# Routing after attention: the order of projection and router products on TensorE, and a reduction split in two on VectorE

## The reference

```python
qkv = (x @ Wqkv + bqkv)                      # 16 heads of 16
scores = q @ k.T / sqrt(16) - slope * |i - j|
x = layernorm(x + softmax(scores) @ v @ Wout + bout)

weights = softmax(x @ router_w.T + router_b)            # 8 experts
topk_vals, topk_idx = top_k(weights, 2)
expert_mask = (topk_flat > 0)[:, :-1]
sorted_indices = argsort(-expert_mask, axis=0)[:cap]    # cap = 512 tokens an expert
inputs = x_flat[used_idx] * sorted_mask
h = relu(inputs @ experts_inter)                        # 256 -> 1024
out = (h @ experts_out) * in_w
x = layernorm(x + scatter_add(out) + x * noop_weight)
```

## Time and profile before

| | |
|---|---|
| median of three executions | 1265.13 us (1259.38 to 1265.17) |
| the profiled execution's own time | 1265.13 us |
| its span, first to last instruction | 1263.2 us |
| mean granted TensorE clock | 0.936 |
| TensorE products busy | 1081.4 us (86%) |
| ScalarE busy | 809.5 us (64%) |
| VectorE busy | 445.3 us (35%) |
| GpSimd busy | 279.4 us (22%) |

### The profile page before, as it was taken

How to read it: one execution, slowest core, us unless ns; L and a number is a source line. 1 busy time by engine, 2 the same in 40 slices (tenths; PEclk the granted TensorE clock), 3 DMA queues, 4 the chain that set the end, 5 groups by cost and what they waited for, 6 DMA issues and landing times. The chain is left out here.

```text
span 1263.2 us, 36424 instructions
## 1 busy us (share of the span) xinstructions
PE 1081.4 (86%) x15545; PEld 699.6 (55%) x15545; DVE 445.3 (35%) x944; ACT 809.5 (64%) x775; POOL 279.4 (22%) x422
## 2 busy tenths in 40 slices
PE   6997299999999999998999999996883599999930
PEld 3554175556576465665557756644772366666630
DVE  3778014443233232253334423223547111111105
ACT  4443299999999999997899999995344111111106
POOL 2322021222212111122211211110801223333210
PEclk9999599999999999998999999998885699999975
DMA  5554623434524222254434342200622234333227
GB/s 176 167 159 124 117 61 67 83 67 82 93 56 87 56 54 49 51 126 86 95 76 76 67 77 54 50 7 21 240 80 87 83 84 100 100 100 101 32 49 234
DMA packets 83304, 112.90 MB, mean 89 GB/s; under 512 B 11376, under 2 KB 69616, under 8 KB 83152
## 3 DMA queue, kind: packets, MB, share of 16 engines
q1 hardware_dynamic: 69328, 94.93, 31.7%
q0 software_dynamic: 5376, 7.34, 3.4%
q10 hardware_dynamic: 8448, 8.39, 2.0%
HBM read 76.45 MB, written 29.98 MB: 84 GB/s over the span
## 5 line engine op out<-in xcount | busy, mean ns | idle before, releaser
L749 ACT ACTIVATE prob<-ps 128x1536 f32<-128x1536 f32 (+4 forms) x504 | 668.4, 1450 | 71.0 <-PE ps L705 69.1
L705 PE MATMUL ps<-q_stack,k_stack 111*32 111x512 bf16 (+13 forms) x6848 | 440.6, 312 | 43.2 <-DMA q_stack<-shift_rows 30.0
L729 PE MATMUL ps<-prob,v_head 128*32 128x128 f32 (+6 forms) x7228 | 443.3, 341 | 7.0 <-issue 6.9
L705 PEld LDWEIGHTS ps<-q_stack,k_stack 111*32 111x32 bf16 (+3 forms) x6848 | 225.1, 97 | 224.2 <-ACT prob L749 107.7
L729 PEld LDWEIGHTS ps<-prob,v_head 128*32 128x32 f32 x7228 | 252.3, 110 | 83.8 <-issue 26.7
L760 POOL TENSOR_TENSOR prob<-prob,near_bias 128x128 f32<-128x128 f32 x256 | 125.6, 494 | 604.7 <-ACT prob L749 604.4
L760 DVE TENSOR_TENSOR prob<-prob,near_bias 128x128 f32<-128x128 f32 x256 | 79.3, 317 | 496.6 <-ACT prob L749 496.5
L778 DVE RECIPROCAL o_rec<-o_den 128x128 f32<-128x128 f32 x128 | 113.0, 923 | 0.6
L1503 PE MATMUL ps<-xeT,w 128*128 128x512 f32 x224 | 99.7, 603 | 5.9 <-ACT xeT L1525 5.9
L1511 PE MATMUL ps<-w,hT 128*128 128x256 f32 x448 | 98.4, 380 | 5.8 <-issue 5.8
L1511 PEld LDWEIGHTS ps<-w,hT 128*128 128x128 f32 x448 | 84.5, 190 | 22.6 <-issue 11.4
(11 more groups left out here) (144 smaller groups left out, 613.2 us busy)
## 6 DMA issues: line engine op xcount, KB each, us to landing
qk_parts<-split SPq DMA_DIRECT2D x96, 128.0 KB
k_stack<-qk_parts SPq DMA_DIRECT2D x32, 384.0 KB
k_stack<-qk_parts SPq DMA_DIRECT2D x32, 256.0 KB
w<-L_ffn_experts_inter_dram SPq DMA_DIRECT2D x7, 1024.0 KB, 5.1
w<-n_L_ffn_experts_out_dram SPq DMA_DIRECT2D x7, 1024.0 KB, 8.2
q_stack<-qk_parts SPq DMA_DIRECT2D x32, 192.0 KB
xin<-in_L_attn_x_dram ACTq DMA_DIRECT2D x8, 512.0 KB, 5.2
q_stack<-qk_parts SPq DMA_DIRECT2D x32, 128.0 KB
```

Source lines behind the costliest of these rows:

```text
L705: mm = pe.matmul(ps[k:k + keys, SLOT_BANKS * (c % 2) + bank, col:col + z - a], k_st[n % STACKS][0:rows, ver, kb * P + k:kb * P + k + keys] ...
L729: mm = pe.matmul(ps[32 * g:32 * g + 32, 6 + n % 2, column:column + width * times], vh[n % 2][:, kb, :], moving, start=g not in begun, stop ...
L749: act.activation(prob[:, c % RING, 0:at + z - a], ps[:, bank:bank + SLOT_BANKS, :].rearrange("p c n -> p (c n)")[:, 0:at + z - a], ACT.Exp ...
```

## The change

The loop that orders TensorE's work is rewritten: `route(n)` is now issued ahead of `project(n + 2)`, where `project(n + 2)` stood ahead of `route(n)`. And the reduction that wrote `place[k]` in bf16 by a maximum now writes `best[k]` in fp32 by a sum, followed by a copy into `place[k]`. `best[k]` is an existing buffer whose earlier contents are no longer read there. Lines behind the first edit are one further down in the changed kernel, and behind the second two.

```diff
@@ -1174,11 +1174,12 @@
                                        rw[:, k, :], start=(k == 0), stop=(k == 1))
                 mm.then_inc(lg_mm, 1)
 
-            for n in range(NCH + 2):
-                if n < NCH:
-                    project(n)
-                if n >= 2:
-                    route(n - 2)
+            project(0)
+            project(1)
+            for n in range(NCH):
+                route(n)
+                if n + 2 < NCH:
+                    project(n + 2)
 
             pe.wait_ge(const, 3)
             pe.wait_ge(mask_done, 1)
@@ -1360,7 +1361,8 @@
                 link(dve.tensor_tensor(mine[:, :, :], in_tile[:, :, :], pick[k][:, :, :], ALU.mult))
-                link(dve.tensor_reduce(place[k][:, :], mine[:, :, :], AX.X, ALU.max))
+                link(dve.tensor_reduce(best[k][:, :], mine[:, :, :], AX.X, ALU.add))
+                link(dve.tensor_copy(place[k][:, :], best[k][:, :]))
```

## The result

The changed kernel takes 1306.33 us (median of four, 1300.34 to 1310.32), the kernel before, run again beside it, 1262.57 us. The ratio is 1.034 with a 95% interval of 1.029 to 1.040: slower, as forecast.

What follows compares the result with a forecast made beforehand. TensorE was taken to bound the routing stage. The new order's waits and low clock add 40.3 us and the reduction 0.4, so 40.7 on 1265.13 gives 1306 us, own range 1300 to 1311.

Steps and rivals of the forecast that it cites:

- The dependence: Routing: chunk n's normalisation sits in VectorE's queue behind chunk n+1's additions, so TensorE waits 3.3 to 3.6 us before transposes.
- The clock: Routing rounds: TensorE's grant falls in each round and returns within the projection, making 10.58 us 13.5.
- The sum: Routing stage, first transposes to last router bias addition: 94.5 us instead of 54.2, 40.3 us more.
- R0: TensorE's transposes and logits of chunk 0 in the routing stage; the number after R is the chunk.
- the tail: End of routing, chunk 6's transposes to the last bias addition: 11.2 us, already at low clock.
- The reduction: Second edit: the reduction itself costs 0, the new cast, run twice, 0.4 us in all, bounds 0 to 0.8.
- a cast that passes GpSimd: VectorE's new cast runs unhindered, using up the next product's wait for GpSimd: cost 0.
- one that is held: VectorE's new cast is held until GpSimd's product ends: about 0.3 us each time, 0.6 us in all.
- The bound on the product behind it: VectorE's product after the cast should end no more than 0.3 us later after GpSimd's end than before.
- A clock that holds: Routing: the grant holds in most new rounds, 10.58 us each, +20.5 us, so 1286; chance 0.13 with mixed cases.
- one that never comes back: Routing: the grant stays low, rounds of 16.0 us, +54 us, so 1319; chance 0.04.
- rival 3: End of routing: only two chunks lack a projection, so the stage gains up to 3.6 us, 1262; chance 0.02.

Runs made afterwards that it cites:

- the kernels with mended queues: Changed kernel with VectorE's scales ahead of the next chunk's additions: 1290.34 us; with ScalarE's evacuation also ahead of the next square root: 1266.68 us.
- the last experiment: Kernel before with later projections between transposes and logits, plus two extra products there in chunks 5 to 7: 1249.93 us, ratio 0.992.

## Why the prediction was right

- **The dependence.** TensorE was to wait 3.3 to 3.6 us in chunks 1 to 6, about 20 us in all; it waited 3.48 and five times 3.17, 19.3 us; the five lie 0.1 us below the range. The way from the second addition to the transposes was put at 3.14 us from the earlier trace rows and is 3.14 (914.77 to 917.91). That it is this way, and no loss of lead as such, the kernels with mended queues show.
- **The clock.** The round was put at 10.58 us for the waits and 13.5 with the clock, plus 0.75 in every second. The last four rounds took 13.7, and 10.57 with work in the wait: 3.1 us a round are the clock, shown by experiment. Two sizes were off and partly cancelled. Low-clock logits took 3.44 us (919.80 to 923.24) and not 3.06, which had been read from a stretch in which the grant fell only after the start: 2.3 us too little over six rounds. The transposes ran low in one round (2.66 us to the logits), not three: 1.5 us too much. How many rounds have this differs between executions; with GpSimd's product later, in the same order of TensorE, the transposes of chunks 0 and 2 were wholly low and those of chunk 1 in part. The first round was 15.34 us, as its whole projection ran at a mean of 0.55, and its way from projection to transposes took 1.5 us more than charged; in the other five it took 0.9 us less in all.
- **The sum.** From R0's transposes to the last bias addition 94.5 us were forecast and 96.3 came: six rounds of 84.7 for 83.3, the tail 11.6 for 11.2. The stage grew by 42.1 us, where 40.3 were forecast. That the median of 1306.33 meets the 1306 forecast so closely is luck: the forecast started from 1265.13 us for the kernel before, whose median beside the changed kernel is 1262.57, so the whole change was +43.8 us for the +40.7 forecast, and the two differences cancel. The four executions of the changed kernel spread over 10 us.
- **The reduction.** 0.4 us were taken, and 2 x 0.2 came, but in part by luck. The 0.4 lay between two cases, 0 for a cast that passes GpSimd and 0.6 for one that is held. The sign to look for was a cast of 0.1 to 0.3 us, the first case, and it took 1.53: the second case came, at 0.2 us each and not 0.3. The Trainium skill states that copies and casts can take the port shared with GpSimd and are then held in full ("SBUF — State Buffer", Who interferes with whom). The trace agrees, with 1.53 us beside GpSimd's product and 0.18 without it. The bound on the product behind it held: it ends 0.75 us after GpSimd, where it ended 0.56 after.
- **The rivals.** A clock that holds would have been 10.6 us a round, one that never comes back 16. The gain in the tail (rival 3) did not come, since the tail stayed at the low clock: the last addition, at 984.27, is 11.6 us after the start of R6's transposes. That such a gain is to be had by other means, the last experiment shows.

## What to carry to other kernels

An order on one engine is only as good as the places of the instructions it waits for on the others: before a producer is moved nearer to its consumer, follow the consumer's operand back through every engine's queue and look for what stands ahead of it that needs the moved work. A lead that looks idle (rows ready 3.5 us early) may be what hides such a place. And where TensorE alternates wide products with narrow ones and waits, price each round at the clock that its poor stretch will leave, and put wide work into gaps, even work that nobody needs, where rows show the grant falling.

## What was not expected of the hardware

- The grant can be low while TensorE is busy without a pause. In the changed kernel the logits, of 8 columns each, keep it occupied for 3.4 us on end at 0.50 (919.80 to 923.20), and in the tail it is busy for 5.54 of 6.30 us at 0.50. With four records of 128x256 more a chunk, between transposes and logits, the grant was 1.00 for 11.8 us.
- Extra work shortened the program: 84 records more on TensorE took 15.0 us off the stage.
- A cast of 128x32 beside GpSimd's product ends with that product, although it moves 32 elements a lane: 1.53 us for 0.18.

The last view, of the tail of the changed kernel:

```profile
978.00:984.30 6.30, 5.54 (x25) 5.05 (x25) 0.22 (x2) 2.68 (x4) 0.00 (x0) 0.50 0.16 53
```
